# Spreading GpSimd's four scalings over four masks in the capped attention of a decoder

## The reference, cut to what matters

```
x = x + _L0_attn_ref(_layernorm(x, axis=-1), L0_attn_Wq, L0_attn_Wk, L0_attn_Wv, L0_attn_Wo)
# in it, per batch b (4) and head h (16), as the kernel computes it:
#   s = 50 * tanh(scale * q k' / 50), set to minus infinity above the diagonal
#   p = exp(s);  o = (p v) / (sum of p);  x += o Wo
```

## Time and profile before

| | us |
|---|---|
| median of three runs | 1279.32 |
| the profiled execution's own time | 1283.95 |
| its span, first to last instruction | 1282.2 |
| PE busy | 1125.2 (88% of the span) |
| DVE busy | 791.8 (62%) |
| ACT busy | 573.8 (45%) |
| POOL busy | 352.6 (28%) |

### The profile page before, as it was taken

The page is one execution under the profiler, slowest core; times in us unless marked ns, Lnnn a source line. Parts: engine busy times, 40 slices in busy tenths (PEclk is TensorE's granted clock), DMA queues, the critical chain, the costliest instruction groups (busy, mean ns, idle before and its releaser), DMA issues. The chain is left out here.

```text
span 1282.2 us, 24467 instructions
## 1 busy us (share of the span) xinstructions
PE 1125.2 (88%) x9243; PEld 693.4 (54%) x9258; DVE 791.8 (62%) x2213; ACT 573.8 (45%) x1193; POOL 352.6 (28%) x416
## 2 busy tenths in 40 slices
PE   5888899878999899899999899988788979994898
PEld 3456544457764444456666455565555545662455
DVE  6732477667588534667886676662333386879855
ACT  3767334663525424364454355324332124547453
POOL 2434303100002200044554222045665203541100
PEclk9888899898989899999999999999999999997999
DMA  9000000000050030000000000534554500000001
GB/s 379 18 1 2 1 1 2 1 1 1 1 202 14 1 132 0 1 1 2 3 2 2 1 2 2 214 118 141 154 151 144 153 10 1 2 3 0 1 1 33
DMA packets 23491, 60.85 MB, mean 47 GB/s; under 512 B 3681, under 2 KB 12009, under 8 KB 22480
## 3 DMA queue, kind: packets, MB, share of 16 engines
q1 hardware_dynamic: 18864, 48.92, 10.8%
q0 software_dynamic: 4512, 10.37, 2.8%
HBM read 52.95 MB, written 8.29 MB: 48 GB/s over the span
## 5 line engine op out<-in xcount | busy, mean ns | idle before, releaser
L860 ACT ACTIVATE PT<-PS 128x384 f32<-128x384 f32 (+1 forms) x320 | 153.2, 531 | 185.8 <-PE PS L673 138.3
L793 DVE CUSTOM_DVE_ANT_0 junk<-PS,TRI 128x128 bf16<-128x128 f32 (+1 forms) x384 | 112.7, 353 | 3.9 <-PE PS L654 0.2
L269 PE MATMUL PS<-identb 128*128 128x512 bf16 x420 | 103.8, 386 | 6.4 <-PEq L626 1.8
L654 PE MATMUL PS<-KS,QM 32*128 32x128 f32 (+1 forms) x768 | 86.7, 347 | 7.5 <-DVE QM L827 6.6
L911 POOL TENSOR_TENSOR OD<-OD 128x256 f32<-128x256 f32 x24 | 17.4, 725 | 272.1 <-DVE OD L832 272.1
L901 POOL TENSOR_SCALAR_AFFINE_SELECT PT<-PT 128x512 f32<-128x512 f32 x96 | 61.0, 635 | 102.9 <-ACT PT L860 102.9
L832 DVE RECIPROCAL OD<-OD 128x256 f32<-128x256 f32 x40 | 69.9, 1747 | 30.9 <-ACT OD L868 25.9
L673 PE MATMUL PS<-QM,KS 32*128 32x256 f32 (+1 forms) x768 | 88.5, 347 | 0.0
L654 PEld LDWEIGHTS PS<-KS,QM 32*128 32x128 f32 x768 | 65.5, 184 | 30.3 <-DVE QM L827 16.7
L742 PE MATMUL PS<-PT,CST 128*32 128x256 f32 (+1 forms) x1280 | 75.4, 353 | 0.0
L2145 PE MATMUL PS<-WU,XT 128*128 x188 | 67.9, 484 | 7.5 <-issue 5.0
(11 more groups left out here) (374 smaller groups left out, 2646.5 us busy)
## 6 DMA issues: line engine op xcount, KB each, us to landing
WD<-w2d_in SPq DMA_DIRECT2D x47, 256.0 KB
WU<-w2u_in SPq DMA_DIRECT2D x1, 5632.0 KB, 17.7
WA<-wl_in SPq DMA_DIRECT2D x1, 5137.0 KB, 15.7
GB<-gate_rows SPq DMA_DIRECT2D x8, 512.0 KB, 8.5
WU<-chosen SPq DMA_DIRECT2D x16, 256.0 KB, 5.5
WB<-wb_in SPq DMA_DIRECT2D x1, 3208.0 KB, 19.2
WA<-wa_in SPq DMA_DIRECT2D x1, 2560.0 KB, 15.3
WA<-w2s_in SPq DMA_DIRECT2D x6, 384.0 KB, 16.8
```

Source lines behind the costliest of these rows:

```text
L269: pe.matmul(PS[:, bank, :].rearrange("p (a n) -> p a n", a=4), identb[:], identb[:].rearrange("p (a n) -> p a n", a=1).to_broadcast([P, 4, ...
L654: return pe.matmul(PS[:, s, m * T:m * T + n], queries(U, v)[rows, m * P:(m + 1) * P], keys(U, v)[rows, 0:n], start=True, stop=True, skip_g ...
L793: last = dve.tensor_tensor_reduce(junk[:, s, m * P:m * T + P], PS[:, s, m * T:m * T + (m + 1) * P], TRI[:, (1 - m) * P:T], 1.0, NEG, ALU.a ...
L860: act.activation(PT[:, g % 3, st_slot(k), 0:W], PS[:, st_bank(g, k), 0:W], ACT.Exp, scale=scale).then_inc(S["at_exp"], 1)
```

## The change

POOL's four scalings of a finished batch, which stood in one block behind the third mask of the next batch, stand behind its third, fourth, fifth and sixth mask, one each: scaling u behind mask `8(b+1) + 2 + u`. The first scaling keeps its place, the last three move behind one, two and three masks. The number of instructions, their operands and their semaphores are the same, and the four scalings of the last batch stay behind mask 31.

```
-                    def scaled(b):
-                        for u in range(UNITS):
-                            g = b * UNITS + u
-                            pool.wait_ge(S["cap_wide"], d["cap_wide"] + g + 1)
-                            pool.wait_ge(S["cap_copied"], d["cap_copied"] + g + 1)
-                            o = QT[:, u, b * T:(b + 1) * T]
-                            pool.tensor_tensor(o, o, RB[:, u, :], ALU.mult).then_inc(S["cap_scaled"], 1)
+                    def scaled(b, u):
+                        g = b * UNITS + u
+                        pool.wait_ge(S["cap_wide"], d["cap_wide"] + g + 1)
+                        pool.wait_ge(S["cap_copied"], d["cap_copied"] + g + 1)
+                        o = QT[:, u, b * T:(b + 1) * T]
+                        pool.tensor_tensor(o, o, RB[:, u, :], ALU.mult).then_inc(S["cap_scaled"], 1)
...
                                            channel_multiplier=-1).then_inc(S["cap_masked"], 1)
-                        if p % 8 == 2 and p >= 8:
-                            scaled(p // 8 - 1)
-                    scaled(B - 1)
+                        if 2 <= p % 8 < 2 + UNITS and p >= 8:
+                            scaled(p // 8 - 1, p % 8 - 2)
+                    for u in range(UNITS):
+                        scaled(B - 1, u)
```

## The result

Six runs of the changed kernel took 1264.81 to 1273.22 us, median **1269.62 us**, beside six of the kernel before with a median of 1280.99 us. The ratio is 0.9909 with a 95% interval of 0.9885 to 0.9933: faster by 0.9%. The forecast was 1269.8 us. The profiled execution took 1264.81 us, for a span of 1263.1 us; it is the fastest of the six, so the 19.1 us between the two spans are not the gain. What the change does has to be read inside the stage.

The account below looks back on a forecast made before the run. PE, held by POOL at batch boundaries, sets the end; elsewhere ACT bounds. Gains of 6.03 + 1.89 + 1.28 + 0.29 = 9.49 us off the 1279.3 us median give 1269.8 us; own range 1268 to 1272, 8 in 10 range 1267.8 to 1274.2.

Parts of the forecast that it names:

- Alternating costs nothing: On POOL, changing between scaling and mask was priced at 0, with 0.7 us per change as the far end.
- Boundary 1: First batch boundary, at product(5): the stall for mask 11 goes and tanh of unit 8 starts 2.41 us earlier.
- Boundary 2: At product(9) and out_product(0): stall gone and both at full clock, gain so far 6.03 us, ACT idle 2.65 us left.
- Boundary 3: At product(13) and out_product(1): stall of 1.89 us gone, plus 1.28 and 0.29 us, sum 9.49 us.
- The tail moves as a whole: End of stage behind product(15): PE's 2.87 us wait for the last reciprocal and the last batch's scalings stay as they stood.
- The waits of the earlier trace: ACT's tanh waited four times for scores, 13.1 us together; one is the stage's start, the others were to be taken singly.
- the clock did not fall anyway: Rival: PE's short waits for tanh still drop the clock, so only the stalls' 5.7 us are won: 1273.6 us, chance 0.13.
- The mask was not late: Rival: POOL changes cost 0.7 us, masks 11, 19, 27 come late, gain 3.9 us: 1275.4, chance 0.08 together with mixtures.
- Nothing was slower: Rival: without the stalls' rest PE's clock stays down over whole units, up to 8.1 us slower, 1287.4 us; chance 0.03.
- The stage's end near 148.3: Sign in the changed trace: the stage ends near 148.3 us in place of 157.8.

Follow-up runs that it names:

- filled stalls: Kernel before, scalings still in one block, with 14 small unread matmuls on PE ahead of product(5), (9) and (13): 1275.62 us, ratio 0.9956.
- out_products spread: Changed kernel with out_product(0) in three pieces behind product(8), (9), (10), and out_product(1) behind product(15), all but one matmul: 1265.01 and 1269.73 us.
- two others: Changed kernel with two scalings behind the third mask, 1272.58 us; kernel before with its whole block of four scalings one mask later, 1270.11 us.

## Why the prediction was right

The mechanism, its place and its size held, step by step:

- *Alternating costs nothing:* right, by the pitches of 0.60 and 0.69.
- *Boundary 1, 2.41 us:* tanh of unit 8 comes 102.42 - 92.03 = 10.39 us behind the scores of unit 5, before 108.72 - 95.90 = 12.82: 2.43.
- *Boundary 2, 6.03 us in all:* scores of unit 12 at 23.69 in place of 29.68: 5.99. ACT's gap 2.63 (forecast 2.65), out_product(0) 115.72 - 112.07 = 3.65 (3.6).
- *Boundary 3, 9.49 us in all:* product(14) at 37.88 in place of 47.35: 9.47.
- *The tail moves as a whole:* not quite. The wait of 2.87 us did, but the spell of half clock behind it came in only half the traces. With 1.69 us for each, half of it is 0.85 us that the sum did not have.
- *The waits of the earlier trace rows:* I named four of ACT's waits and took two. The third, 1.72 us at unit 3, follows the half clock of the first units; it is 0.56 us in the changed trace, by chance of when the clock rose.
- *The rivals:* the clock did not fall anyway: it was 1.00 over more than 44 us. So the rule of the Trainium skill, "TensorE: Matmul & The Clock Gate", section "A second HAM failure mode: psum-queue depth-cycling", did not come true for this pattern, in which PE idles in short pieces and cycles through banks. That rival's price of 5.7 us was also too high: the filled stalls show 4.99, since part of the first stall falls where PE would have waited for a tanh anyway. The mask was not late. Nothing was slower.
- *The stage's end near 148.3:* it came near 142.7. The stage began 2.7 us earlier in that trace, its first units got the full clock 1.2 us sooner, and the tail kept it, 1.7 us.

That the forecast of the total came within 0.2 us is luck: it took 2 us too little off a base that was 1.7 to 1.9 us too low. The median of the 58 runs of the kernel before that stand beside the changed one's is 1281.2 us, not 1279.3, and 1281.2 - 1269.5 is 11.7 us. Of these 9.47 are shown in the stage, 0.85 are the tail's if so few traces can be trusted, and 1.4 stay open. The traces point to the clock in the first units (13.9 to 15.2 us to the scores of unit 5 in the changed kernel's, 15.2 to 16.0 before) and behind the stage (1118.9 to 1122.7 us, and 1120.1 to 1123.6 before), but seven traces are too few to call that an effect of the change.

## What to carry to other kernels

Where one engine serves two consumers in program order, look at which item the bound engine needs next and put the bulk that nobody waits for behind that item; its length matters less than what stands behind it. Price a stall of PE twice, for the wait and for the matmuls behind it at half clock, and then ask whether PE has slack before its next deadline: the stall of 0.58 us ahead of product(5) was made up by the scores of unit 10. When a wait is filled to keep the clock, look for the next fall behind it before you count the gain. And measure a stage by a distance between two fixed instructions in it: here that told 9.47 us to 0.1, where medians of six runs told 11 give or take 3.

## What the runs showed of the hardware

- Three idle spells of PE of 1.9 us were each followed by a little over 3 us at 0.50 of the clock in all three traces of the kernel before. Filled to 0.25 us of idle, or left at 0.5 us, none was; nor was the idle of 1.07 us ahead of product(14) with the out_products spread.
- The spell behind an idle time of 2.87 us is not certain: it came in six of the ten traces that kept this wait (three of three before, two of four changed, one with filled stalls, none of two others).
- Without that idle time the clock stayed at 1.00 through the tail, in four of four traces, and fell some 13 us into the next stage, at a cost of 1.5 us (three traces) or 3.15 us (one). In the ten others it did not fall within 25 us there.
- The same code behind the stage took 1115.9 to 1128.4 us; the mean clock from 700 to 840 us behind the stage was 1.00 in the shortest trace, and 0.95 and 0.96 in the two longest.
- Changing between mask and scaling on GpSimd costs nothing: the pitch is 0.60 us behind a mask and 0.69 behind a scaling when they alternate, and 0.59 and 0.685 in a row of masks or of scalings.
